# Slots of 122 rows instead of 128 for the routed feed-forward items of an adaLN block

## What is computed

```python
h = _layernorm(x, axis=-1) * (1 + ca) + sa
x = x + ga * _L0_attn_ref(h, Wq, Wk, Wv, Wo)
h = _layernorm(x, axis=-1) * (1 + cb) + sb
# _L0_ffn_ref
probs = jax.nn.softmax(x @ router_w.T, axis=-1)
w = _top_p_weights(probs, TOP_P)
for e in range(n_exp):
    g = jax.nn.silu(x @ gate_w[e].T)
    u = x @ up_w[e].T
    y = g * u @ down_w[e].T
    out = out + y * w[:, e:e + 1]
# back in the block
x = x + gb * _L0_ffn_ref(h, ...)
```

## Time and profile before

| | us |
|---|---|
| median of 3 runs | 493.86 |
| lowest and highest | 489.47, 495.75 |
| profiled execution, its own time | 491.9 |
| its span, first to last instruction | 490.3 |

### The profile page before, as it was taken

One profiled execution on the slowest core, in us unless ns is written; L12 is line 12 of the kernel. 1 busy time (PEld: TensorE's weight loads), 2 busy tenths in 40 slices (PEclk: granted clock), 3 DMA queues, 4 the chain that ended last, 5 costly groups with the idle time before them and its releaser, 6 DMA issues. The chain is left out here.

```text
span 490.3 us, 10014 instructions
## 1 busy us (share of the span) xinstructions
PE 457.1 (93%) x3466; PEld 349.2 (71%) x3466; DVE 334.5 (68%) x790; ACT 258.9 (53%) x358; POOL 199.1 (41%) x235
## 2 busy tenths in 40 slices
PE   7978989998999999999999799999989999999992
PEld 7373343454535445345899799989979999999992
DVE  3597786499767976768898768557437585665542
ACT  3237878767776788677452245344226353524230
POOL 4142033013100200004235667566756666676755
PEclk8899999999999999999999899999999999999998
DMA  8601203901010100223334547757537556565443
GB/s 258 225 1 45 87 2 30 128 16 43 2 45 1 44 1 11 79 87 111 109 127 114 128 92 171 198 111 192 89 68 177 131 128 158 117 119 111 78 77 45
DMA packets 30785, 46.01 MB, mean 94 GB/s; under 512 B 3588, under 2 KB 22276, under 8 KB 30728
## 3 DMA queue, kind: packets, MB, share of 16 engines
q0 software_dynamic: 11936, 22.50, 25.9%
q1 hardware_dynamic: 18792, 22.77, 14.1%
HBM read 34.44 MB, written 12.93 MB: 97 GB/s over the span
## 5 line engine op out<-in xcount | busy, mean ns | idle before, releaser
L645 ACT ACTIVATE probs<-psS 128x1024 f32<-128x1024 f32 x128 | 123.1, 1028 | 21.4 <-PE psS L1487 21.1
L1730 PE MATMUL psS<-hs_hi,w_hi 128*128 128x256 f32 x400 | 113.1, 283 | 3.0 <-issue 2.3
L1730 PE MATMUL psS<-hs_lo,w_hi 128*128 128x256 f32 x400 | 112.4, 281 | 0.0
L1730 PE MATMUL psS<-hs_hi,w_lo 128*128 128x256 f32 x400 | 112.3, 281 | 0.0
L506 POOL DMA_INDIRECT out<-y_sel,idx_out x44 | 76.7, 1744 | 35.8 <-DVE y_sel L1293 22.7
L1730 PEld LDWEIGHTS psS<-hs_hi,w_hi 128*128 128x128 f32 x400 | 75.3, 188 | 4.1 <-issue 4.1
L1730 PEld LDWEIGHTS psS<-hs_lo,w_hi 128*128 128x128 f32 x400 | 75.3, 188 | 0.0
L1730 PEld LDWEIGHTS psS<-hs_hi,w_lo 128*128 128x128 f32 x400 | 75.3, 188 | 0.0
L492 POOL DMA_INDIRECT h_sel<-h_rows,idx_in x50 | 55.8, 1115 | 43.7 <-DVE sel L1259 19.3
L1594 PE MATMUL psY<-probs,v_aug 128*32 128x512 f32 x512 | 68.2, 605 | 0.0
L697 ACT ACTIVATE silu_g<-psS 128x512 f32<-128x512 f32 x50 | 29.8, 598 | 59.2 <-PE psS L1730 58.8
(11 more groups left out here) (224 smaller groups left out, 736.7 us busy)
## 6 DMA issues: line engine op xcount, KB each, us to landing
w_in<-gateT SPq DMA_DIRECT2D x8, 512.0 KB, 4.8
w_in<-upT SPq DMA_DIRECT2D x8, 512.0 KB, 4.5
w_in<-downT SPq DMA_DIRECT2D x8, 512.0 KB, 4.7
h_rows<-h_nat SPq DMA_DIRECT2D x4, 528.0 KB, 3.1
x_all<-x SPq DMA_DIRECT2D x4, 512.0 KB, 5.2
h_rows<-mod_table POOLq DMA_DIRECT2D x4, 512.0 KB, 15.0
out<-x_all SPq DMA_DIRECT2D x4, 512.0 KB, 2.9
mod_rows<-mod_table SPq DMA_DIRECT2D x3, 512.0 KB, 5.7
```

The costliest lines, as they stand in the source:

```text
L645: act.activation(probs[:, gk % 4, 2 * pair:2 * pair + 2, :], psS[:, pair, :, :], ACT.Exp, scale=ATT_SCALE).then_inc(probs_done, 1)
L1730: mm = pe.matmul(ps[:, i * SW:(i + 1) * SW], w, v[:, k, :], start=at == 0, stop=at == 3 * KC - 1)
```

## The change

A slot holds PR = 122 rows, an item 244, and the lists have TSLOTS = 2 * ceil(2048 / 244) = 18 slots. Gathers, scatters, weighing and turns take rows 0 to 121. The matmuls of gate and up stream 244 columns, ACT and DVE work on 488 elements where they had 512. Since 122 is no power of two, the slot is found as round((rank - 60.5) / 122), rounding by adding and subtracting 1.5 * 2**23, and the row as rank - 122 * slot, in floating point; early_places is changed like places (not shown). The number of items is found in the same way. 18 x 122 is more than 2048, so the last item that an expert can have is not full to its end with places of tokens: when an expert reaches it (its 9th item, the 7th for experts 0 and 1), DVE puts zeros for its spare rows' weights (clear_places) and POOL takes the places of an earlier item for them (replace_places). On POOL and DVE walk_items has a compare for this in its loops. The 12 matmuls on kT become 12 more turns of the identity.

```diff
@@ -52,11 +52,15 @@
-    TSLOTS = T // P
+    PR = 122
+    TSLOTS = S * -(-T // (S * PR))
-    SW = S * P
+    SW = S * PR
+    ROUND = 1.5 * 2.0 ** 23
...
@@ -270,7 +271,7 @@
-            return (psY, psM)[j][:, 1, 0:C] if last else psY[:, 0, j * C:(j + 1) * C]
+            return (psY, psM)[j][0:PR, 1, 0:C] if last else psY[0:PR, 0, j * C:(j + 1) * C]
...
@@ -281,13 +282,21 @@
-        def walk_items(eng, body, between):
+        def last_item(e):
+            return (T - (SLOTS0 * PR if e < EXPERTS0 else 0)) // SW
+        def walk_items(eng, body, between, fullest=None):
+                            if fullest:
+                                with eng.If(i > last_item(e) - 1):
+                                    fullest(e, before + i)
...
@@ -296,6 +305,9 @@
+                            if fullest:
+                                with eng.If(n + i > end + last_item(e) - 1):
+                                    fullest(e, first + i)
...
@@ -414,7 +426,7 @@
-            pool.memset(early_most[:, 0:EXPERTS0], float(SLOTS0 * P)).then_inc(zeroed, 1)
+            pool.memset(early_most[:, 0:EXPERTS0], float(SLOTS0 * PR)).then_inc(zeroed, 1)
...
@@ -445,7 +457,7 @@
-            pool.iota(token_f[:, :, :], [[P, NT], [0, E]], base=0, channel_multiplier=1, **small).then_inc(consts, 1)
+            pool.iota(token_f[:, :, :], [[P, TILES0], [0, EXPERTS0]], base=0, channel_multiplier=1, **small).then_inc(consts, 1)
...
@@ -489,8 +501,8 @@
-                    pool.indirect_dma_start(h_sel[:, k, :], None, h_rows[0:rows, :],
-                                            bass.IndirectOffsetOnAxis(ap=idx_in[:, k:k + 1], axis=0)).then_inc(gathered, 16)
+                    pool.indirect_dma_start(h_sel[0:PR, k, :], None, h_rows[0:rows, :],
+                                            bass.IndirectOffsetOnAxis(ap=idx_in[0:PR, k:k + 1], axis=0)).then_inc(gathered, 16)
...
@@ -503,8 +515,8 @@
-                    pool.indirect_dma_start(out_rows[0:rows, :], bass.IndirectOffsetOnAxis(ap=idx_out[:, k:k + 1], axis=0),
-                                            sums[:, k, :], None, compute_op=ALU.add).then_inc(scattered, 16)
+                    pool.indirect_dma_start(out_rows[0:rows, :], bass.IndirectOffsetOnAxis(ap=idx_out[0:PR, k:k + 1], axis=0),
+                                            sums[0:PR, k, :], None, compute_op=ALU.add).then_inc(scattered, 16)
...
@@ -545,7 +557,29 @@
-            walk_items(pool, body_of_item, lambda e, before: None)
+            replaced = ctx.enter_context(pool.register("replaced"))
+            pool.reg_mov(replaced, 0)
+            def replace_places(e, m):
+                left = (T - (SLOTS0 * PR if e < EXPERTS0 else 0)) % SW
+                pool.wait_ge(consts, NCONST)
+                pool.wait_ge(in_listed, m)
+                pool.wait_ge(gathered, 32 * (m + 1))
+                pool.wait_ge(scattered, GATES + 32 * (m - 2))
+                pool.tensor_copy(idx_all[left:PR, bass.ds(S * m, 1)],
+                                 idx_all[left:PR, bass.ds(S * (m - 2), 1)]).then_inc(places_replaced, 1)
+                pool.reg_add(replaced, replaced, 1)
+                pool.wait_ge(places_replaced, pool.snap(replaced, min_val=1, max_val=S * E))
+                pool.sem_inc(replace_seen, 1)
+                pool.tensor_copy(idx_all[0:PR, bass.ds(S * m + 1, 1)],
+                                 idx_all[0:PR, bass.ds(S * (m - 2) + 1, 1)]).then_inc(places_replaced, 1)
+                pool.reg_add(replaced, replaced, 1)
+                pool.wait_ge(places_replaced, pool.snap(replaced, min_val=S, max_val=S * E))
+                pool.sem_inc(replace_seen, 1)
+            walk_items(pool, body_of_item, lambda e, before: None, replace_places)
...
@@ -689,12 +723,12 @@
-                act.copy(hs_hi[:, :, :].rearrange("p k t -> p (k t)"), psM[:, 0, :]).then_inc(sel_hi, 1)
+                act.copy(hs_hi[:, :, :].rearrange("p k t -> p (k t)"), psM[:, 0, 0:KC * SW]).then_inc(sel_hi, 1)
-                act.activation(silu_g[:, h, :], psS[:, 0, h, :], ACT.Silu).then_inc(silu_ready, 1)
+                act.activation(silu_g[:, h, :], psS[:, 0, h, 0:2 * SW], ACT.Silu).then_inc(silu_ready, 1)
...
@@ -984,9 +1018,6 @@
-            dve.wait_ge(ident_done, 1)
-            for half in range(2):
-                dve.tensor_copy(kT[:, 1, 0, half * P:(half + 1) * P], ident[:, :]).then_inc(awake_in, 1)
...
@@ -1209,15 +1239,14 @@
-                step(dve.tensor_tensor(rank_i[:, :, :], fill[:, :, :], ranks, ALU.add))
+                step(dve.tensor_tensor(rank_f[:, :, :], fill[:, :, :], ranks, ALU.add))
-                dve.tensor_scalar(tile_i[:, :, :], rank_i[:, :, :], 7, None, ALU.arith_shift_right).then_inc(rt_step, 1)
-                at[0] += 1
-                step(dve.tensor_scalar(row_i[:, :, :], rank_i[:, :, :], P - 1, None, ALU.bitwise_and))
-                dve.tensor_copy(tile_h[:, :, :], tile_i[:, :, :]).then_inc(rt_step, 1)
-                at[0] += 1
-                step(dve.tensor_copy(row_h[:, :, :], row_i[:, :, :].rearrange("p t e -> p e t")))
+                step(dve.tensor_scalar(tile_f[:, :, :], rank_f[:, :, :], (PR - 1) / 2.0, 1.0 / PR, ALU.subtract, ALU.mult))
+                step(dve.tensor_scalar(tile_h[:, :, :], tile_f[:, :, :], ROUND, ROUND, ALU.add, ALU.subtract))
+                step(dve.scalar_tensor_tensor(out=row_h[:, :, :], in0=tile_h[:, :, :].rearrange("p t e -> p e t"),
+                                              scalar=float(-PR), in1=rank_f[:, :, :].rearrange("p t e -> p e t"),
+                                              op0=ALU.mult, op1=ALU.add))
...
@@ -1234,10 +1263,10 @@
-                step(dve.tensor_scalar(count_i[:, :], count_f[:, :], float(SW - 1), None, ALU.add))
-                step(dve.tensor_scalar(meta[:, 0, :], count_i[:, :], 8, None, ALU.logical_shift_right))
-                step(dve.tensor_scalar(meta[:, 0, :], meta[:, 0, :], 1.0, None, ALU.max))
-                step(dve.tensor_copy(count_f[:, :], meta[:, 0, :]))
+                step(dve.tensor_scalar(before_f[:, :], count_f[:, :], (SW - 1) / 2.0, 1.0 / SW, ALU.add, ALU.mult))
+                step(dve.tensor_scalar(before_f[:, :], before_f[:, :], ROUND, ROUND, ALU.add, ALU.subtract))
+                step(dve.tensor_scalar(count_f[:, :], before_f[:, :], 1.0, None, ALU.max))
+                step(dve.tensor_copy(meta[:, 0, :], count_f[:, :]))
...
@@ -1250,20 +1279,20 @@
-                dve.tensor_tensor(hs_lo[:, :, :].rearrange("p k t -> p (k t)"), psM[:, 0, :],
+                dve.tensor_tensor(hs_lo[:, :, :].rearrange("p k t -> p (k t)"), psM[:, 0, 0:KC * SW],
-                dve.tensor_scalar(sel[:, bass.ds(m % RING, 1), :, 1:].rearrange("p o k e -> p (o k) e"), h_sel[:, :, C:ROW], 0.0,
+                dve.tensor_scalar(sel[0:PR, bass.ds(m % RING, 1), :, 1:].rearrange("p o k e -> p (o k) e"), h_sel[0:PR, :, C:ROW], 0.0,
-                dve.tensor_tensor(a_full[:, h, :], psS[:, 1, h, :], silu_g[:, h, :], ALU.mult).then_inc(a_ready, 1)
+                dve.tensor_tensor(a_full[:, h, :], psS[:, 1, h, 0:2 * SW], silu_g[:, h, :], ALU.mult).then_inc(a_ready, 1)
...
@@ -1287,10 +1316,10 @@
-                    row = sel[:, bass.ds(m % RING, 1), k, :].rearrange("p a c -> p (a c)")
+                    row = sel[0:PR, bass.ds(m % RING, 1), k, :].rearrange("p a c -> p (a c)")
-                    weighed = dve.scalar_tensor_tensor(out=into[:, k, :], in0=down_rows(k, last),
+                    weighed = dve.scalar_tensor_tensor(out=into[0:PR, k, :], in0=down_rows(k, last),
...
@@ -1378,7 +1407,21 @@
-            walk_items(dve, body_of_item, between_experts)
+            cleared = ctx.enter_context(dve.register("cleared"))
+            dve.reg_mov(cleared, 0)
+            def clear_places(e, m):
+                left = (T - (SLOTS0 * PR if e < EXPERTS0 else 0)) % SW
+                dve.wait_ge(w_copied, m + 1)
+                of = sel[:, bass.ds(m % RING, 1), :, 1:1 + E].rearrange("p o k e -> p (o k) e")
+                dve.tensor_scalar(of[left:PR, 0, :], ident[left:PR, 0:E], 0.0, None, ALU.mult).then_inc(weights_cleared, 1)
+                dve.tensor_scalar(of[0:PR, 1, :], ident[0:PR, 0:E], 0.0, None, ALU.mult).then_inc(weights_cleared, 1)
+                dve.reg_add(cleared, cleared, S)
+                dve.wait_ge(weights_cleared, dve.snap(cleared, min_val=S, max_val=S * E))
+                dve.sem_inc(clear_seen, 1)
+            walk_items(dve, body_of_item, between_experts, clear_places)
...
@@ -1567,12 +1610,7 @@
-            stay_awake(18)
-            pe.wait_ge(awake_in, 2)
-            for cols in (P, 2 * P - 12, 2 * P):
-                for _ in range(4):
-                    pe.matmul(psS[:, 1, 1, 0:cols], kT[:, 1, 0, 0:P], kT[:, 1, 0, 0:cols], start=True, stop=True)
+            stay_awake(30)
...
@@ -1711,8 +1749,8 @@
-                        mm = pe.transpose(psM[:, 0, k * SW + j * P:k * SW + (j + 1) * P], h_sel[:, j, k * P:(k + 1) * P],
```

(24 more changed lines are left out.)

20 lines of the change are left out of this document (7 added, 13 removed).

## The result

The change makes the kernel slower by 40%: 687.75 us (four runs, 686.17 to 691.89) against 493.11 for the kernel before in the same comparison, ratio 1.4035 (95% interval 1.3983 to 1.4087). The profiled execution has a span of 684.6 us, 194.3 more than the earlier trace rows.

What follows compares the result with a forecast made beforehand. PE, busy 93% of the span, was taken as the bound. Terms -7.1 - 0.3 + 0.75 + 1.5 - 0.2 (tail) = -5.35 us took 491.9 to 486.5; with 2.0 for the median, 488.5 us, range 484 to 495.

Steps and rivals of the forecast that it cites:

- rival 1: Gathers and scatters: 122 rows dealt to 2 engines, 61 each, landings 9.0 us later, about 625 us; chance 0.13.
- 122 rows instead of 128 might save up to 5% of a DMA: Gathers and scatters: fewer rows save up to 5% of a DMA, offsetting some stalls, counted only in the ends.
- a dealer that rounds up: Argument against few queues: rows dealt rounding up, 8 on most engines, so 122 rows cost nothing.
- the completion in 16 parts: Argument against few queues: a DMA's completion still comes in 16 parts.
- Gate and up matmuls: Walked items on PE: 244 columns instead of 256 save 7 ns a matmul, 7.1 us; ends 5.0 and 9.1.
- Rival 4: Gate and up on PE: the 244-column rate doesn't carry over, 5 ns or less, -2 us, 491.5; chance 0.1.
- Stalls of late gathers: PE waiting for h_sel: less slack in POOL's round adds 1.5 us of stalls, ends 0 and 4.
- The longer loop: Fourth item's loop: 18 slots bring one more empty pass on PE's path, +0.75 us, "issue" gap near 3.05 us.
- Number of items: Gate and up groups: 25 items, 4 early and 21 walked, unchanged; the gain is in shorter items, not fewer.
- Early items: Before 275 us: four items, mostly held by the fifth gather's wait on DVE, -0.3 us; ends +0.7 and -1.3.
- Down matmuls and turns: Walked items on PE: no change, 0; new column offsets at most 1 us either way over 21 items.
- The sum: All terms together: -5.35 us, from a profiled 491.9 us to 486.5, forecast as 488.5 on the median.

## Why the prediction was wrong

I forecast 488.5 us and put 484 to 495 around it; it took 687.75. The mechanism was on the page as rival 1, with a chance of 0.13.

- **The step that failed.** In the sum the DMAs stood as "122 rows instead of 128 might save up to 5% of a DMA": a price by bytes. It is set by the rows in the largest share: a gather's landing grew 4.4 us, a scatter's 7.4, and their issues by 0.6 and 1.3. With them the round through the scatters, 7.4 us before and hidden behind PE's 9, became 16.55 and set the pace. I gave most weight to a dealer that rounds up and to the completion in 16 parts. The second is no evidence: 124 and 122 rows complete by the same count of 16. The first was an assumption, against the rule of the Trainium skill (DMA: Bandwidth & Descriptors) that I had quoted; the rule held, as the counts of packets above show.
- **The range.** It left rival 1 out, although "it decides as soon as a gather lands over 2.6 us later than now". With a rival 130 us away and nothing in the trace that excludes it, the chances could say so and the range could not.
- **The rival's size.** 625 us where 687.75 was measured. I took 0.17 us a packet and 53 packets more in a gather, but a gather's packet holds two rows: 4.4 us, not 9.0. Then I followed the gathers' loop only. The scatters' loop is longer (two issues in a row, then landing and y_sel), 16.55 us a round against my 15.5, and the loss before and behind the walk and the lower clock were not in my product of 21 items.
- **Gate and up matmuls.** I took 7 ns of 119; with 128-row DMAs it is 4.9 (118.8 to 113.9), 4.9 us of my 7.1; in the kernel before alone it is 5.5 outside the item at half clock. The three matmuls in a row at 26 us had said 0.113 us against 0.119, which the walk bears out; I took 0.112. Rival 4's cap of 5 ns was nearer than the forecast, but its own sum was off: with 5 ns mine gives -3.3 us, not -2. The 2.5 ns that I worked out by the Trainium skill (TensorE: Matmul & The Clock Gate, "Back-to-back issue gap") were too few: the runs show 4.9 and 5.5.
- **Stalls of late gathers.** 1.5 us, measured 1.5 (4.7 for 3.2) with 244 columns alone. With both DMAs at 128 rows the total is 4.0, but in the walk it is 2.9 for 0.7, 2.2 more: the wait ahead of the walk shrank at the same time.
- **The longer loop.** +0.75; 2.3 to 3.0 us of "issue", right.
- **Number of items.** 25, right: the gate and up groups have 400 matmuls each.
- **Early items.** I took 0.3 us. With both DMAs at 128 rows PE takes 55.9 us from the first turn to the sixth, 57.1 in the unchanged kernel: 1.2 us, near my end of 1.3.
- **Down matmuls and turns.** I took 0, and 1 us for what new offsets might do. Down matmuls are 1 ns apart (118.0 for 119.0), 0.5 us. The 1 us was a slip: 6 ns on 28 matmuls in 21 items are 3.5.
- **The sum.** From -5.35, a total of +0.9 (interval -0.1 to +2.6) is a miss of 6 us. The rate explains 2.2 of it, late gathers and PE's waits for hs_lo 0.7 each, the granted clock up to 2.4, and the early items were 0.9 better than I took; over 1 us stays open, and none of the profiles can tell it from the spread.

## What to carry to other kernels

Before the rows of an indirect DMA are changed, factor the count: the largest divisor up to 16 says how many engines carry it. A count with a bad divisor cost far more than the work that it saved (122: 194 us, 124: 80), while 126 cost some 1 us. If an odd tile size is wanted for the matmuls, keep the DMA at a good count with spare rows, or choose the tile by the DMA. And where a kernel has rings of DMAs beside the bound engine, price a change of their length for each ring, the one through the scatters too.

## What I had not expected

- POOL's issue of an indirect DMA grows as the engines get fewer, 1.74 to 3.07 us for a scatter and 1.12 to 1.77 for a gather, with fewer rows in it. By the counts above a scatter of 122 rows has 61 packets for each of 16 engines, 976 where 128 rows have 128; that the issue grows with them fits, and wasn't tried.
- Uneven counts come with packets of 8 bytes that did not exist before: on average 13 a DMA at 126 rows, 276 at 124, 637 at 122, 8 ns each. Their numbers are those of fillers for the engines without a share; what they are for is open.
- A stall can cost more than its length: with PE waiting 5 us an item the granted clock was 0.81 in place of 1.00, which put 49 us on PE's own busy time, and a single gap of 2.3 us was followed by 3.4 us at half clock, another 1.7 us.
- Removing three of four empty passes, and a gap of 2.3 us with them, made the kernel 3.2 us slower, by the ratio, with gaps at items whose own code was not changed.
